# Attention block on one core: which engine computes the low parts of the probabilities

## Time and profile before

| what | us |
| --- | --- |
| median of the three runs | 3899.88 |
| the profiled execution, whole | 3898.04 |
| its span, first to last instruction | 3896.3 |
| PE busy (98% of the span) | 3821.6 |
| ACT busy (78%) | 3023.8 |
| DVE busy (69%) | 2674.6 |
| POOL busy (51%) | 1982.4 |

### The profile page before, as it was taken

One profiled execution on the slowest core, in us unless ns is written; L12 is line 12 of the kernel. 1 busy time (PEld: TensorE's weight loads), 2 busy tenths in 40 slices (PEclk: granted clock), 3 DMA queues, 4 the chain that ended last, 5 costly groups with the idle time before them and its releaser, 6 DMA issues.

```text
span 3896.3 us, 97290 instructions
## 1 busy us (share of the span) xinstructions
PE 3821.6 (98%) x39180; PEld 3138.6 (81%) x39180; DVE 2674.6 (69%) x4387; ACT 3023.8 (78%) x5141; POOL 1982.4 (51%) x1022
## 2 busy tenths in 40 slices
PE   7999999999999999999999999999999999999998
PEld 5888788887888878888888888878888788787886
DVE  6776667666676676667766676676766766766665
ACT  6887878778787787877878788787887877878776
POOL 2454544545445464454644546455454544545444
PEclk9999999999999999999999999999999999999999
DMA  3021111211112121121211211112111110111111
GB/s 93 20 54 43 55 47 26 58 37 55 47 26 64 34 55 47 26 66 29 56 47 29 69 26 53 47 35 65 26 53 47 45 56 25 51 49 43 50 26 52
DMA packets 100723, 178.50 MB, mean 46 GB/s; under 512 B 16192, under 2 KB 16192, under 8 KB 100288
## 3 DMA queue, kind: packets, MB, share of 16 engines
q1 hardware_dynamic: 100288, 172.29, 16.0%
HBM read 71.57 MB, written 33.55 MB: 27 GB/s over the span
## 4 chain that ended last, share of the span: by engine, by line
PE 89%; ACT 3%; issue 2%; POOL 2%; DVE 2%; DMA 1%; SPq 0%; ACTq 0%; DVEq 0%; POOLq 0%
PE psum L555 36%; PE psum L574 13%; PE psum L606 11%; PE psum L608 11%; PE psum L628 6%; PE psum L632 6%; PE psum L630 5%; PE psum L564 1%; POOL xT_lo L465 1%; ACT p_hi L709 1%; POOL p_lo L471 1%; DVE max_parts L809 1%; PE psum L582 1%; ACT p_full L708 1%; ACT q_hi_hi L691 0%
## 5 line engine op out<-in xcount | busy, mean ns | idle before, releaser
L471 POOL TENSOR_TENSOR p_lo<-p_full,p_hi 128x1024 f16<-128x1024 f32 x768 | 1646.7, 2144 | 1739.2 <-ACT p_hi L709 1739.2
L708 ACT ACTIVATE p_full<-psum,prob_bias 128x512 f32<-128x512 f32 x2048 | 1429.5, 698 | 633.7 <-PE psum L608 624.0
L809 DVE TENSOR_REDUCE max_parts<-psum 128x1 f32<-128x512 f32 x2048 | 1377.1, 687 | 708.7 <-PE psum L574 702.6
L709 ACT ACTIVATE p_hi<-psum,prob_bias 128x512 f16<-128x512 f32 x2048 | 1425.9, 696 | 0.0
L628 PEld LDWEIGHTS psum<-v_parts,p_hi 128*128 128x128 f16 x8192 | 744.2, 98 | 239.5 <-issue 149.7
L574 PE MATMUL psum<-k_lo_hi,q_hi_hi 128*128 128x512 f32 x2048 | 850.3, 436 | 14.2 <-DMA q_hi_hi<-q_hi_hi 6.4
L628 PE MATMUL psum<-v_parts,p_hi 128*128 128x65 f16 x8192 | 858.2, 193 | 4.3 <-POOL p_lo L471 2.7
L630 PE MATMUL psum<-v_parts,p_hi 128*128 128x64 f16 x8192 | 852.1, 192 | 0.0
L632 PE MATMUL psum<-v_parts,p_lo 128*128 128x65 f16 x8192 | 849.7, 194 | 0.0
L606 PE MATMUL psum<-q_hi_hi,k_lo_hi 128*128 128x512 f32 x2048 | 807.4, 394 | 19.4 <-DVE q_shift L819 16.3
L608 PE MATMUL psum<-q_shift,k_shift 128*128 128x512 f32 x2048 | 802.3, 392 | 0.0
(11 more groups left out here) (66 smaller groups left out, 4714.9 us busy)
## 6 DMA issues: line engine op xcount, KB each, us to landing
q_hi_hi<-q_hi_hi SPq DMA_DIRECT2D x256, 128.0 KB, 2.2
k_shift<-k_lo_hi SPq DMA_DIRECT2D x256, 128.0 KB, 2.2
y_tile<-in_x SPq DMA_DIRECT2D x125, 256.0 KB, 2.7
result<-y_tile SPq DMA_DIRECT2D x125, 256.0 KB, 2.0
x_in<-in_xT SPq DMA_DIRECT2D x121, 256.0 KB, 2.9
o_heads<-in_L_conv_w_qkv SPq DMA_DIRECT2D x12, 256.0 KB, 4.4
p_full<-in_xT SPq DMA_DIRECT2D x4, 256.0 KB, 5.1
o_heads<-in_L_conv_w_out SPq DMA_DIRECT2D x4, 256.0 KB, 3.2
```

The source lines that it names most:

```text
L471: nc.gpsimd.tensor_tensor(p_lo[:, g % LO_SLOTS, :, :], p_full[:, g % 2, :, :], p_hi[:, g % HI_SLOTS, :, :], ALU.subtract).then_inc(p_lo_re ...
L708: nc.scalar.activation(p_full[:, g % 2, n, :], scores(g, n), ACT.Exp, scale=SCALE, bias=prob_bias[:, :])
L709: nc.scalar.activation(p_hi[:, g % HI_SLOTS, n, :], scores(g, n), ACT.Exp, scale=SCALE, bias=prob_bias[:, :]).then_inc(exp_done, 1)
L809: nc.vector.reduce_max(max_parts[:, u % 2, q_tile, k_half:k_half + 1], bank(b, w), AX.X).then_inc(done["row_max"], 1)
```

## The change

The table of steps whose low part POOL computes gets the two missing entries, so that POOL computes all of them and DVE none.

```diff
-POOL_STEPS = (0, 1, 2, 4, 5, 6)
+POOL_STEPS = (0, 1, 2, 3, 4, 5, 6, 7)


 def on_pool(s):
     return s % 8 in POOL_STEPS
```

## The result

The changed kernel takes 3909.71 us (median), the kernel before 3899.88: ratio 1.0024, 95% interval 1.0016 to 1.0032, so about 10 us slower, clear of noise and far below two per cent (13 runs of each; the one of 9526.74 us is left out of the ratio). The profiled execution has a span of 3907.5 us, 11.2 more than before.

The account below looks back on a forecast made before the run. PE, busy 98% of the span, was taken as the bound. Terms 1.3 + 6.8 + 2.2 = 10.3 us on the profiled 3898.04 gave 3908.3; with the median 1.8 higher, 3909 was named, range 3898 to 3922.

Parts of the forecast that it names:

- The place decides, not the sum over the span: Whole kernel: only room before single low parts' readers, and places where POOL's queue is full, decide; busy totals decide nothing.
- The price of a moved low part: Each moved low part: 2.143 us on POOL against 1.226 on DVE; POOL rises from 1982 to some 2530 us.
- Slot 43, 1.3 us: Slot 43, all 16 images: the low part ends later on POOL, PV starts 0.08 us late; 1.3 us in all.
- Slots 47 to 51, 6.8 us: POOL's full queue delays input tile 3, so slot 51's v fill starts 0.52 us later in 13 images: 6.8 us.
- The cover of PV(49): PV of step 49 comes 0.28 us late at no cost, since the next matmul stood waiting anyway.
- The 14 us foreseen for PE's wait for the input's low part: Slot 51's fill: PE's total wait for POOL's input low part was to grow from 7.3 to some 14 us.
- the rival on ACT: Slots 47 to 51: tile 3's late load idles ACT 0.3 us; about 0.8 more in 15 images, 3915 to 3924; chance 0.15.
- The 13 of 15: Slot 51: of 15 images with a successor, PE waited for POOL's input tile 3 in 13, so 0.52 was counted 13 times.
- The tail, 2.2 us: Last image, slots 54 to 61: POOL's unbroken eight low parts and six bias additions, 24.3 us, delay PV(60) by 2.2 us.
- DVE gives nothing back: DVE's relief costed at nothing: weight loads' 9.7 us of waits for row maxima are mostly no idle time of PE.
- The bounds that were named, 3890 to 3915: Whole kernel's time by the low and high ends of the single terms alone: 3890 to 3915 us.
- POOL's rival: Low parts after slot 53 start late too, up to 0.9 us per slot: 70 us, 3980; chance 0.05, shared with anything unseen.

Follow-up runs that it names:

- the stand-in: Changed kernel plus a DVE maximum over 1024 constants at each moved low part's place, restoring DVE's load: 3908.75 us, ratio 1.0026 to the kernel before.

## Why the prediction was right

The time came within 0.7 us of the 3909 that was named. That closeness is partly luck, as the interval of the difference runs from 6.2 to 12.5 us; the parts below are what bears the account.

**The place decides, not the sum over the span.** Right: 16 of the 64 low parts of an image were moved and two of them cost, with the tail of the last image. Putting those back alone restored the old time, with 221 others still moved.

**The price of a moved low part.** Right: 2.145 us on POOL, as on the rows of before; 2502 us busy where 2530 were said, since the 120 input tiles got shorter by 24 us in all and rows overlap in a full queue.

**Slot 43, 1.3 us.** Right, slightly small: 0.11 in place of 0.08 per image by the median, 1.5 us over all 16.

**Slots 47 to 51, 6.8 us.** Right: the stretch is 0.50 longer, 6.4 us over the 15 images, and the fill starts 11.52 to 11.54 us after step 47's second exp in all of them, where it was 11.01 to 11.03 in the 13 images that waited before. The cover of PV(49) held. Two things under it were different.

The 14 us foreseen for PE's wait for the input's low part did not come: it grew from 7.3 to 10.7. The matmul in front of the fill came later as well. It starts 0.10 after the low part of k on DVE in every image of both traces, and that one waits for ACT. Before and after:

```profile
2145.61 0.76 DVE L792 SCALAR_TENSOR_TENSOR k_lo_hi<-psum,qk_bias,k_lo_hi 64x512 fp32r<-64x512 f32 x1 [0.61 <-ACT k_lo_hi L693]
```

```profile
2150.15 0.76 DVE L792 SCALAR_TENSOR_TENSOR k_lo_hi<-psum,qk_bias,k_lo_hi 64x512 fp32r<-64x512 f32 x1 [0.92 <-ACT k_lo_hi L693]
```

ACT's input tiles 2 and 3 took 1.42 us in this trace where they took 1.19, as tile 3's load came late:

```profile
2146.26 1.42 ACT L661 CAST xT_hi<-x_in 128x512 fp32r<-128x512 f32 x2
```

That is the rival on ACT, 0.2 to 0.3 us as it said. POOL's tile 3 came later still and hid it, as the prediction counted: the fill starts at the same time in images where the matmul in front of it comes at 10.12 and where it comes at 10.95. The rival's further 0.8 us per image did not appear.

The 13 of 15 was an accident of the trace of before. In the other two images tile 3's load landed 4.5 us after its issue (2.9 in the median), and PE lost 0.55 us there to ACT already before the change:

```profile
1662.82 0.62 ACT L661 CAST xT_hi<-x_in 128x512 fp32r<-128x512 f32 x1 [1.19 <-DMA x_in<-in_xT]
...
1664.66 0.50 PE L606 MATMUL psum<-q_hi_hi,k_lo_hi 128*128 128x512 f32 x1 [1.20 <-ACT p_hi L709]
```

After the change all 15 images have the same 38.13, so these two did not move. With no late load before, the sum would have been 15 x 0.5 = 7.5; what a late load costs is the rival on ACT at work.

**The tail, 2.2 us.** Right: 2.16, with POOL's chain at 24.20 us where the layout had 24.3, and the moved bias additions gave 3.66 back for 3.7.

**DVE gives nothing back.** Right, and shown by the stand-in: the weight loads' waits for the row maxima went from 9.7 to 2.1 us and came back to 8.9 without a trace in the time.

**What was missing.** The 1.6 us of the clock in one of the last fills were not in the sum. They are in both profiles of the changed kernel and not in that of before, but other runs show that they come and go with neither the change nor the tail. Without them the sum of the parts is 10.1, for 10.3 predicted. The bounds that were named, 3890 to 3915, lack the 1.8 us by which the median was put above the profiled execution; nothing hangs on it.

**POOL's rival** (low parts late after slot 53 too) did not happen: the stretch from step 56 to the next image's step 40 is 183.93 us before and 183.92 after; it repeats to 0.13 (183.79 in the second profile of the changed kernel), and the rival asked for up to 4.5 per image.

## What to carry to other kernels

When work moves between two engines that are both off the bound, lay the receiving queue out again, instruction by instruction, only at the places where its reader has no cover, and skip the totals: here two of sixteen moved instructions per image and a few in the last image made all of the loss. The same layout tells where to move work the other way: taking one low part of 64 out of the full stretch gave back 0.98 us per image, more than the whole change cost there (0.50). And an idle time of the weight loads need not be one of the matmuls: try it by putting the load back.

## What the runs showed of the hardware

- A DVE subtraction with both inputs in SBUF lasts 1.226 us alone and mostly 1.7 to 2.2 us beside POOL's, and POOL's input tile 2.09 beside it instead of 1.29; both vanish when one of them is gone. Once, beside a full POOL queue, it lasted 4.40: it started during one POOL instruction and ended only after the next two, which were not lengthened. A DVE maximum over 1024 constants from SBUF (1.209 to 1.222 us in its 256 runs beside a busier POOL) is not lengthened.
- In a full POOL queue the next start comes about 0.03 to 0.05 us before the row of the one in front ends (2.10 between starts for rows of 2.14).
- Two profiles of the same program drifted apart by 2.0 us over 3900, evenly over the images, while the three stretches of the table, from step 40 to 46, 46 to 56 and the tail, agreed to 0.02 us: short stretches of like position compare far better than spans.
